# A decoder kernel: operands made inside the tiled attention's block, small parts of the maxima on GpSimd, last weights loaded during a norm

## The reference, cut to what matters

```
x = x + msa(layernorm(x, ln1_w, ln1_b), w_qkv, w_proj)
x = x + moe_mlp(layernorm(x, ln2_w, ln2_b), gate_w, gate_b, w1, w2)
```

```
xe, xo = x[..., ::2], x[..., 1::2]
real = xe * cos - xo * sin
imag = xe * sin + xo * cos
```

## Time and profile before

| | |
|---|---|
| median of three runs | 2487.46 us (2482.86 to 2488.14) |
| profiled execution: its own time | 2489.26 us |
| its span, first to last instruction | 2487.4 us |
| busy in the span | PE 2246.2, ACT 1618.2, DVE 988.4, PEld 749.3, POOL 473.5 us |
| mean granted TensorE clock | 0.945 |
| rotary operands to the end of the rotary attention | about 878 to 1236 us |
| last block's first norm, operands and attention | about 2053 to 2331 us |

### The profile page before, as it was taken

One profiled execution on the slowest core, in us unless ns is written; L12 is line 12 of the kernel. 1 busy time (PEld: TensorE's weight loads), 2 busy tenths in 40 slices (PEclk: granted clock), 3 DMA queues, 4 the chain that ended last, 5 costly groups with the idle time before them and its releaser, 6 DMA issues. The chain is left out here.

```text
span 2487.4 us, 30101 instructions
## 1 busy us (share of the span) xinstructions
PE 2246.2 (90%) x12042; PEld 749.3 (30%) x12042; DVE 988.4 (40%) x1516; ACT 1618.2 (65%) x1234; POOL 473.5 (19%) x210
## 2 busy tenths in 40 slices
PE   6899999589979988898989999999999976899897
PEld 2333333144436632222211111111111111233365
DVE  5766775125441156767221111111211115787112
ACT  1999889423332222454479999999999962566433
POOL 0577765401100032555400000000000000000000
PEclk9899999889989987999989999999999996999999
DMA  1000000046643011000010010010000000000010
GB/s 41 5 9 5 5 1 1 1 153 214 210 165 141 17 27 43 1 1 1 1 44 1 1 41 1 1 42 1 1 1 1 1 1 9 1 1 1 20 34 25
DMA packets 28989, 78.93 MB, mean 32 GB/s; under 512 B 3584, under 2 KB 18832, under 8 KB 26784
## 3 DMA queue, kind: packets, MB, share of 16 engines
q1 hardware_dynamic: 15032, 30.91, 4.3%
q0 software_dynamic: 4384, 29.56, 3.4%
q10 hardware_dynamic: 9448, 16.70, 1.9%
HBM read 71.62 MB, written 5.59 MB: 31 GB/s over the span
## 5 line engine op out<-in xcount | busy, mean ns | idle before, releaser
L1672 ACT ACTIVATE crat_E<-banks 128x1536 f32<-128x1536 f32 x544 | 749.4, 1461 | 22.0 <-PE banks L1572 8.2
L1588 PE MATMUL banks<-crat_E,crat_vst 128*32 128x512 f32 x3264 | 437.2, 608 | 0.2 <-ACT crat_E L1672 0.2
L1572 PE MATMUL banks<-crat_Q,mid_arena 52*128 52x512 bf16 x1632 | 329.6, 386 | 21.3 <-ACT crat_E L1672 17.1
L1699 DVE COPY crat_vst<-all_crossV 128x96 f32<-128x96 f32 x136 | 34.3, 252 | 642.0 <-PE banks L1588 641.8
L1320 ACT ACTIVATE rotat_E<-banks 128x1024 f32<-128x1024 f32 x128 | 124.0, 1021 | 166.9 <-PE banks L1208 166.7
L427 POOL TENSOR_TENSOR dist_wsum<-dist_wsum,dist_D 128x1024 f32<-128x1024 f32 x92 | 217.3, 2362 | 8.2
L345 DVE TENSOR_SCALAR dist_D<-banks,dist_k 128x512 f32<-128x512 f32 x256 | 178.5, 747 | 52.0 <-PE banks L213 52.0
L1364 DVE TENSOR_REDUCE rotat_mx<-banks 128x1 f32<-128x512 f32 x256 | 164.1, 685 | 74.5 <-PE banks L1179 71.8
L1572 PEld LDWEIGHTS banks<-crat_Q,mid_arena 52*128 52x128 bf16 x1632 | 60.2, 93 | 443.2 <-ACT crat_E L1672 318.4
L1320 ACT ACTIVATE lastat_E<-banks 128x1024 f32<-128x1024 f32 x128 | 123.9, 1020 | 99.3 <-PE banks L1200 99.3
L1364 DVE TENSOR_REDUCE lastat_mx<-banks 128x1 f32<-128x512 f32 x256 | 164.2, 685 | 40.7 <-PE banks L1179 36.9
(11 more groups left out here) (251 smaller groups left out, 2766.5 us busy)
## 6 DMA issues: line engine op xcount, KB each, us to landing
mlp_M<-in_mask POOLq DMA_DIRECT2D x28, 800.5 KB
mid_arena<-cross_k SPq DMA_DIRECT2D x42, 204.0 KB
moe_W<-in_experts SPq DMA_DIRECT2D x16, 512.0 KB, 3.6
mid_arena<-in_rot_tables ACTq DMA_DIRECT2D x8, 1024.0 KB, 18.2
mlp_C<-in_ctx SPq DMA_DIRECT2D x17, 384.0 KB, 4.6
cross_k<-mlp_kp ACTq DMA_DIRECT2D x17, 288.0 KB, 2.3
mlp_row<-in_mask POOLq DMA_DIRECT2D x1, 3202.0 KB, 12.7
mlp_M<-in_mask POOLq DMA_DIRECT2D x1, 3202.0 KB
```

Source lines behind the costliest of these rows:

```text
L1572: last = pe.matmul(PS[:, 3 * (at % 2) + k, :], K[s:s + ROWS, 2 * (g % 2) + pair, c * P:(c + 1) * P], Q[s:s + ROWS, 2 * g + pair, qh * HALF ...
L1588: last = pe.matmul(PS[32 * j:32 * j + 32, 6 + ps % 2, :], vst[:, (ps * STEPS + c // 3) % 3, c % 3, j, :], E[:, at // 3 % NE, at % 3, :], s ...
L1672: act.activation(flat(E[:, at % NE, :, :]), flat(PS[:, 3 * (at % 2):3 * (at % 2) + 3, :]), ACT.Exp, scale=CROSS_SCALE).then_inc(s_e, 1)
```

## The change

1. The two functions for operands become classes, `RotaryOperands` and `PlainOperands`, whose parts run inside the tiled attention's block. The rotary one makes four products, then four times one product and eight looks. `A` lies in the ring `E`; V uses banks 6 and 7. The loads for the cross attention's tiles wait for the last multiplication with a table.
2. The last block's operands are made in the same way; the second K goes, all masked K come from ScalarE, its V copy stays on VectorE. Its four weight loads are issued in the norm before.
3. `maxima` is one reduction over 32 values on VectorE (in the last block with one more operation). The parts are six dependent operations on GpSimd (`parts`), behind its third addition of a pass.
4. The turn moves into tile 7, ahead of `values`; the lag is 6 in passes 1 to 6.

```diff
-def rotary_operands(nc, PS, name, x, pre, Q, K, Qb, Kb, V, wo):
+class RotaryOperands:
+    AHEAD = 4
+    STEPS = 2 * GROUPS - AHEAD
...
+    def product(self, pe, i):
+        PS, pre, o = self.PS, self.pre, self.ORDER[i]
+        if i == 0:
+            pe.wait_ge(pre.s_in, pre.LOADED)
+        for eo in range(2):
+            if i:
+                pe.wait_ge(self.s_ta, 2 * i - 1 + eo)
+            for h in range(2):
+                last = pe.matmul(PS[:, 2 * eo + h, :], pre.W[:, o, eo * P:(eo + 1) * P], half(self.x, h),
+                                 start=True, stop=True)
+            last.then_inc(self.s_eo, 1)
+        if i >= 2:
+            pe.wait_ge(self.s_vals, i - 1)
+        pe.matmul(PS[:, 6 + i % 2, :], self.x[:, i * P:(i + 1) * P], pre.wv[:, :], start=True, stop=True
+                  ).then_inc(self.s_prod, 1)
...
+    def tensor_first(self, pe):
+        for i in range(self.AHEAD):
+            self.product(pe, i)
+        pe.wait_ge(self.s_cast, 2)
...
+        act.wait_ge(self.s_ta, 4 * GROUPS)
+        self.early.early_scalar(act)
...
+    def sync(self, sp):
+        sp.wait_ge(self.s_ta, 4 * GROUPS)
+        self.early.early_sync(sp)
...
+class PlainOperands:
+    STEPS = 1
...
+    def tensor_first(self, pe):
+        PS, W, x = self.PS, self.W, self.x
+        pe.wait_ge(self.s_w, 64)
+        for o, at in ((0, 0), (1, 2)):
...
+        last.then_inc(self.s_v, 1)
+        pe.wait_ge(self.s_low, 2)
...
+    def scalar(self, act):
...
+        act.activation(self.Qb[:, 0, :], q, ACT.Copy).then_inc(self.s_low, 1)
+        act.activation(self.Kb[:, 0, :], k, ACT.Copy, scale=rows[:, 0, 0:1]).then_inc(self.s_low, 1)
+        act.activation(self.Q[:, 0, :], q, ACT.Copy).then_inc(self.s_q, 1)
+        for j in range(GROUPS):
+            act.activation(self.K[:, j, :], k, ACT.Identity, scale=rows[:, 0, j:j + 1], bias=rows[:, 1, j:j + 1]
+                           ).then_inc(self.s_k, 1)
+            if j:
+                act.activation(self.Kb[:, j, :], k, ACT.Copy, scale=rows[:, 0, j:j + 1]).then_inc(self.s_low, 1)
...
-        return 0 if ps in (-1, 0, LAST) else 8 if ps == 1 else 4
+        return 0 if ps in (-1, 0, LAST) else 6
...
                 pe.wait_ge(s_set, 3 if pairs else 2)
-                for at in range(LOOKS):
-                    look(at)
+                operands.tensor_first(pe)
+                each = LOOKS // operands.STEPS
+                for i in range(operands.STEPS):
+                    operands.tensor(pe, i)
+                    for at in range(i * each, (i + 1) * each):
+                        look(at)
                 turn(0)
+                operands.tensor_done(pe)
...
+                        if c == NT - 1 and ps < LAST:
+                            turn(ps + 1)
                         if c:
                             values(ps, c - 1)
...
-                        if ps < LAST and (ps, c) == turned(ps + 1):
-                            turn(ps + 1)
...
+                def parts(ps):
+                    pool.wait_ge(s_top, ps + 1)
+                    if ps:
+                        pool.wait_ge(s_mu, turn_slot(ps - 1) + 1)
+                    own.up(pool.tensor_scalar(mr[:, 1, :, :], top[:, ps % 2, :, :], -1.0, None, ALU.mult))
+                    own.done()
+                    own.up(pool.tensor_copy(part_of(0), mr[:, 1, :, :]))
+                    own.done()
+                    own.up(pool.tensor_tensor(mr[:, 0, :, :], mr[:, 1, :, :], part_of(0), ALU.subtract))
+                    own.done()
+                    own.up(pool.tensor_copy(part_of(1), mr[:, 0, :, :]))
+                    own.done()
+                    own.up(pool.tensor_tensor(mr[:, 1, :, :], mr[:, 0, :, :], part_of(1), ALU.subtract))
+                    own.done()
+                    pool.tensor_copy(part_of(2), mr[:, 1, :, :]).then_inc(s_mb, 1)
...
+                if pairs:
+                    parts(0)
                 for ps in range(PASSES):
...
+                        if pairs and k == 2 and ps < LAST:
+                            parts(ps + 1)
...
-                    own.up(dve.tensor_tensor(mr[:, 0, :, :], mx[:, 0, :, :], mx[:, 1, :, :], ALU.max))
-                    own.done()
+                    dve.tensor_reduce(top[:, ps % 2, :, :], mx[:, :, :, :], AX.X, ALU.max).then_inc(s_top, 1)
+                    dve.wait_ge(s_top, ps + 1)
+                    if pairs:
+                        return
...
-            plain_operands(nc, PS, "lastop", normed, a, Q, K, Qb, Kb, vst, wproj, sel, rows)
+            operands = PlainOperands(nc, inner, PS, normed, a, Q, K, Qb, Kb, vst, wproj, sel, rows)
+            layer_norm(nc, PS, "lastn1", onesd, x, normed, scale=cols[:, 2:3], shift=cols[:, 3:4], early=operands)
```

More of the change, by code:

```diff
@@ L455, in layer_norm, with _ @@
         with nc.Block() as block:
+            if early is not None:
+                @block.sync
+                def _(sp):
+                    early.early(sp)
             @block.vector
@@ L948, in early @@
             eng.dma_start(self.C[:, o, :, :], a["rot_tables"][o]).then_inc(self.s_in, 16)
-def rotary_operands(nc, PS, name, x, pre, Q, K, Qb, Kb, V, wo):
+class RotaryOperands:
     ORDER = [o for g in range(GROUPS) for o in (g, GROUPS + g)]
[L957 to L1014, removed]
-                for i, o in enumerate(ORDER):
-                    pool.wait_ge(s_ta, 2 * i + 2)
-                    pool.tensor_tensor(result(o), A[:, i % 2, 0, :], A[:, i % 2, 1, :], ALU.add).then_inc(s_sum, 1)
-                pool.wait_ge(s_sum, 2 * GROUPS)
-                pool.wait_ge(s_wo, 1)
@@ new lines, in tensor, with tensor_done, vector_first, vector @@
+    def tensor(self, pe, i):
+        self.product(pe, self.AHEAD + i)
+    def tensor_done(self, pe):
+        pe.wait_ge(self.s_cast, 2 * GROUPS)
+        pe.wait_ge(self.s_vals, NT)
+        pe.wait_ge(self.s_wo, 1)
+    def vector_first(self, dve):
+        for i in range(self.AHEAD):
+            self.turn(dve, i)
+    def vector(self, dve, i):
+        self.turn(dve, self.AHEAD + i)
+    def scalar(self, act):
+        for i, o in enumerate(self.ORDER):
+            if i == NT - 2:
+                act.wait_ge(self.s_wo, 1)
+            act.wait_ge(self.s_prod, i + 1)
+            act.activation(self.V[:, i, :], self.PS[:, 6 + i % 2, :], ACT.Copy).then_inc(self.s_vals, 1)
+            act.wait_ge(self.s_sum, i + 1)
+            act.activation(self.low(o), self.result(o), ACT.Copy).then_inc(self.s_cast, 1)
+        act.wait_ge(self.s_ta, 4 * GROUPS)
+        self.early.early_scalar(act)
@@ L1087, in tiled_attention @@
+def tiled_attention(nc, PS, name, operands, Qs, Ks, Qbs, Kbs, stationary, scale, wo, H, ident, sel=None, rows=None, ES=None,
                     spare=None):
@@ L1128, in tiled_attention @@
         ones = n.sb("ones", [P, 32])
-        mx = n.sb("mx", [P, 2, 4, 4])
+        mx = n.sb("mx", [P, 4, 4, 2])
+        top = n.sb("top", [P, 2, 4, 4])
         mr = n.sb("mr", [P, 2, 4, 4])
+        operands.scratch(E)
         if pairs:
@@ L1160, in tiled_attention, with _ @@
         with nc.Block() as block:
-            if early is not None:
-                @block.sync
-                def _(sp):
-                    early.early_sync(sp)
+            @block.sync
+            def _(sp):
+                operands.sync(sp)
             @block.tensor
@@ L1291, in _ @@
             def _(act):
-                if early is not None:
-                    early.early_scalar(act)
+                operands.scalar(act)
                 nc.scalar.preload_act_table_set("natural_log_exp_and_others")
@@ L2058, in decoder @@
                 layer_norm(nc, PS, "ln3", onesd, x, x, Y=0)
-                rotary_operands(nc, PS, "rotop", x, pre, wide, K, Qb, Kb, V, wo)
+                operands = RotaryOperands(nc, inner, PS, x, pre, wide, K, Qb, Kb, V, wo, tiles)
                 tail = Arena(arena)
```

161 lines of the change are left out of this document (83 added, 78 removed).

## The result

The changed kernel takes 2445.95 us in the median of four runs (2444.05 to 2453.01); the kernel before, on the same chip, 2485.38. The ratio is 0.9846, 95% interval 0.9823 to 0.987. The forecast was 2455 (2441 to 2472).

A forecast was written before the change was run, and what follows sets the result against it. At pass boundaries a VectorE operation held by GpSimd's addition delays the turn, costing 5.77 us a pass. Terms -1 + 20.5 + 1 + 1.5 + 8.2 + 2 = 32.2 off 2487.46 give 2455.3 us, range 2441 to 2472.

The forecast's parts named there:

- rival B: Pass boundaries: GpSimd's addition holds the new VectorE reduction too, only 8.5 us saved in five, 2467 us; chance 0.06.
- Boundaries: Five boundaries of passes 1 to 6: excess 1.7 us instead of 5.77, 4.1 saved each, 20.5 in all.
- T: Time of the six small GpSimd operations at a pass boundary, taken as 1.8 us, bounds 1.0 and 3.9.
- First boundary: Into pass 1: VectorE operation not held, only its five successors leave VectorE's queue; +1 us, bounds 0 to +4.
- Merged rotary block: Rotary operands and first maxima in one block: interleaving gain against slow-clock products; -1 us, bounds -3.2 and +5.8.
- A: Rival: clock stays up through the first block's looks, which gains 5.8 us instead of losing 1, 2448 us; chance 0.10.
- Into pass 7: Last boundary, without looks: tile 7's scores run ahead of the turn, parts 0.7 later; +1.5 us, -1 to +3.
- Last attention's start: Weights' loads move into the norm, four matmuls and the block change go; first reduction 8.2 us earlier, 7 to 9.3.
- Last attention's boundaries: No GpSimd additions there, nothing held; a later turn saves waits for reductions, +2 us, -2 to +3.6.
- C: Rival: small GpSimd operations cost 0.65 us each; gain 33.0 - 7T is 5.7 at T = 3.9, 2482 us; chance 0.05.
- D: Rival: slower than before; gain gone at 0.78 us per small GpSimd operation, 2505 us at 1.2 each; chance 0.04.
- E: Rival: first use of an operation on GpSimd stalls, 7.7 us for two new kinds, 2463 us; chance 0.05.

The follow-up runs named there:

- a_twice: Changed kernel with the six GpSimd operations of the parts done twice over, same values: 2469.26 us.
- b_reduce: Kernel before with only the join of the maxima's halves made one reduction, the five small operations staying on VectorE: 2482.54 us.
- b_parts: Kernel before with the new maxima, GpSimd parts, lag and turn in both attentions, operands and loads left in place: 2449.99 us, ratio 0.9864.
- a_dveparts: Changed kernel with the small operations of the parts back on VectorE; merged blocks, lag and late turn kept: 2482.62 us.
- a_held: Changed kernel with the semaphores of the last attention and its operands cleared only after the norm that follows: 2446.39 us, ratio 0.9828.
- a_ahead7: Changed kernel with seven of the merged rotary block's eight products before the first look, only the eighth among the looks: 2446.81 us.
- a_fine: Changed kernel with half a product between two pairs of looks in the merged rotary block: 2441.8 us, ratio 0.9817.
- a_latew: Changed kernel with the last attention's weights loaded in its own merged block, not in the norm ahead: 2447.52 us.
- a_turn6: Changed kernel with the turn back at the end of tile 6 and the lag 4: 2471.46 us.
- a_oneclear: Changed kernel with the operands' and the attention's semaphores cleared in one block, at both attentions: 2445.51 us, ratio 0.984.

## Why the prediction was right

The forecast was 9 us too high. The main mechanism stood, the hold and its price at a boundary, and most terms were too small; the reason given against rival B was wrong, a stage that lost 3.4 us was missing, and part of the agreement at the boundaries is luck.

*Boundaries, +20.5 forecast, 24.8 measured.* The held VectorE operation and its price were read rightly, and T was forecast at 1.8 and is 1.83. What was mis-sized is the excess of 1.7 us a pass that was to remain: it is 30.93 - 30.12 = 0.81. I had charged 1.0 of waiting, 0.3 for the turn's transposes and 0.4 for a clock that falls now and then. TensorE did wait (0.91) and the transposes took 0.31 to the next product, 1.2 together; 0.4 of it comes back in the tiles around, and the rows don't say where. The clock never fell at these boundaries, and that is luck: in five of the seven other kernels with the same 0.91 us it fell at one of the five, for 1.5 us, an average of 0.2 a pass over all forty. The price of a fallen clock, 2.2 in the working for the high bound, was too high. a_twice shows that the edge is near: 1.95 us more, and all five passes pay.

*The hold (rival B).* The reduction took 0.19 us under the addition: B is dead. My reason against it, one input instead of two, does not hold though: b_reduce shows an operation with one input held for 3.64 us. Had the change put only the first operation elsewhere, the hold would have moved one place on and little would be left (b_reduce's five passes take 179.26 against 179.45).

*First boundary, +1 forecast, 4.8 measured in pass 0.* The bound of +4 "if the clock then stays up" is what happened. b_parts has it too (42.1 us) and a_dveparts, merged but with the parts on VectorE, has not (47.47), so it belongs to the parts. It isn't certain in every execution: a_held and a_ahead7 took 47.2 and 47.3 us, the length before, not by a fall at the turn but by a low clock at the start of the pass that lasted 12 us longer, counted from the first scores (about 25 us instead of 12.6). What decides that is open.

*Merged rotary block, -1 forecast, +2.5 measured.* The clock did fall behind each stretch of looks, at 909, 919 and 930 us, as the next product began, so A did not happen. The mis-sized term is 3.0 for each slow product: they took 5.40, 5.40 and 5.08 instead of 3.60, 1.8 at most and 5.1 in all instead of 9.0, since the clock fell late and came back within the product. The steps were shorter too, 8.86 where the clock held against 9.3 in the forecast. a_fine shows that the fall was avoidable.

*Into pass 7, +1.5 forecast, 2.3 measured. Last attention's start, 8.2 forecast, 8.6 measured,* of which 3.0 is the early load (a_latew). The memset took 1.80 as estimated; the norm itself ran 1.0 slower (its first four products took 3.75 instead of 2.46), so the operands gained 9.6, a little more than the upper bound.

*Last attention's boundaries, +2 forecast.* The attention gained 3.4 (2.8 of it in the first pass; a_ahead7, with the same instructions there, shows only 0.3 of that, 39.38 against 39.71) and the stage behind it lost 3.4. That stage was no term of the sum: the price of taking the operands' block into the attention's, a second clearing behind it, was overlooked, as was what 0.8 us more of idle time does to the next norm's clock.

*Rivals C, D, E.* The operations cost 0.23 to 0.26 us, about 0.3 with their wait: no C, no D. The slope in C, 7 us for each us of T, is too low beyond the edge: a_twice lost 23 us for 1.95, which is 12 for each, since the clock goes as well. Its total at T = 3.8 is nevertheless 13 us better than C's 2482 (T = 3.9). At that price the five boundaries were to gain about nothing, and a_twice's still gain 6.8 (172.6 against 179.45), since a lost clock costs 1.5 and not 2.2; pass 0 is 4.0 shorter than before as well. Where C's 33.0 comes from the prediction doesn't show; from its own terms (11.7 outside the five boundaries, less 2.1 twice) the gain at T = 3.9 would be 7.5 and not 5.7. E: GpSimd's first TENSOR_SCALAR and CAST took 0.26 and 0.25 us:

```profile
941.73 0.26 POOL L1378 TENSOR_SCALAR rotat_mr<-rotat_top 128x16 f32<-128x16 f32 x1 [2.92 <-DVE rotat_top L1429]
942.06 0.25 POOL L1380 CAST rotat_mb<-rotat_mr 128x16 bf16<-128x16 f32 x1
```

The first follows VectorE's reduction, its last input, by 0.09 us (941.64 to 941.73), so there is no stall at a first use here. The Trainium skill (GPSIMD Engine Reference, Instruction dispatch) gives about 6 us for the first call of freshly loaded code; no row shows it, and whether these operations' code was freshly loaded no row shows either. The Trainium skill (GPSIMD Engine Reference, Engine selection) puts elementwise work on VectorE. The bare durations agree, 0.18 to 0.20 us there against 0.23 to 0.26, but the choice doesn't hold at this place, where VectorE is held for 3.64 in front of them.

## What to carry to other kernels

Where a tiny operation takes as long as another engine's big one, moving only that operation passes the hold to the next: look which of its successors would be held too, and move the whole chain, above all to the engine that it waited for anyway. Then put the point where TensorE needs the result behind other work, and count how much idle time is left there: here 0.91 us mostly cost only itself (the clock fell at 5 of 40 boundaries), 2.2 us cost the clock at four of five (a_turn6), and 2.75 us at all five (a_twice). When blocks are merged, read also what stands behind them (clearing, barriers), and interleave in pieces small enough that TensorE does not do the thin work alone for long, as a_fine does.

## What the hardware showed that was not expected

- VectorE's tensor_scalar from f32 to bf16 with one SBUF input was held for 3.64 us by a GpSimd addition, in two kernels, while a TENSOR_REDUCE from SBUF took 0.19 under the same addition.
- At a pass boundary TensorE's idle time of 0.91 us was followed by a granted clock that stayed up at 35 boundaries and fell at 5. After 2.21 it stayed up once and fell four times (a_turn6), and after 2.75 and 2.78 it was down. Ahead of the norm behind the last attention it was up after 1.32 (a_held) and 1.81 (before) and down after 2.33 (a_oneclear) and 2.62. Ahead of the norm behind the rotary attention the same idle time of 2.84 was followed by slow products (3.63 us for four) in the changed kernel and by fast ones (1.98) in a_held, and with the code of before 2.23 by slow ones (3.59, before) and 2.24 by fast ones (1.98, b_reduce). So the last idle time alone does not decide.
- The low stretch at the start of the rotary passes ended 12.6 us behind the first scores in the changed kernel (near 957) and 24.6 in a_held (near 967), with the same instructions around it. In the length of pass 0 this is worth about 5 us (42.38 against 47.15).
